# Filter pass of a four-layer graph network: attributes as three bf16 parts, bf16 transposes and first layer, index loads that wait for gathers

## The reference

```python
def _L2_gnn_ref(x, edge_index, edge_attr, W1, b1, W2, b2, Ws, bs, Wn, bn):
    src, dst = (edge_index[0], edge_index[1])
    h = jax.nn.relu(edge_attr @ W1.T + b1)
    w = h @ W2.T + b2
    msg = w * x[src]
    agg = jax.ops.segment_sum(msg, dst, num_segments=x.shape[0])
    return jax.nn.relu(x @ Ws.T + bs + agg @ Wn.T + bn)
```

## Time and profile before

| | us |
|---|---|
| median of three runs (8740.71 to 8760.54) | 8757.48 |
| the profiled execution's own time | 8686.3 |
| its span, first to last instruction | 8684.5 |
| TensorE busy | 5822.4 (67%) |
| VectorE busy | 4301.2 (50%) |
| POOL busy | 3273.6 (38%) |
| ScalarE busy | 1758.3 (20%) |

### The profile page before, as it was taken

The page is one execution under the profiler, slowest core; times in us unless marked ns, Lnnn a source line. Parts: engine busy times, 40 slices in busy tenths (PEclk is TensorE's granted clock), DMA queues, the critical chain, the costliest instruction groups (busy, mean ns, idle before and its releaser), DMA issues. The chain is left out here.

```text
span 8684.5 us, 135899 instructions
## 1 busy us (share of the span) xinstructions
PE 5822.4 (67%) x29812; PEld 4117.1 (47%) x29813; DVE 4301.2 (50%) x14700; ACT 1758.3 (20%) x3520; POOL 3273.6 (38%) x3354
## 2 busy tenths in 40 slices
PE   4313666794555554555454778888878888889999
PEld 4312443573333333333332455555555555677877
DVE  7877777424666666666666233333333333432222
ACT  0013888202111111111112111111111111110000
POOL 0105000004555555555552555555555555300000
PEclk9856777897777777777777566556665656689999
DMA  1231332553333333333332222222222222256666
GB/s 31 102 100 61 107 103 100 187 221 75 71 72 70 71 69 71 71 70 71 71 69 31 43 34 34 35 34 35 35 34 34 35 35 35 23 207 246 255 240 232
DMA packets 1052581, 764.66 MB, mean 88 GB/s; under 512 B 868977, under 2 KB 978241, under 8 KB 1032914
## 3 DMA queue, kind: packets, MB, share of 16 engines
q1 hardware_dynamic: 664738, 483.03, 18.4%
q0 software_dynamic: 131808, 243.11, 11.8%
q10 hardware_dynamic: 255904, 37.09, 2.5%
HBM read 657.77 MB, written 143.22 MB: 92 GB/s over the span
## 5 line engine op out<-in xcount | busy, mean ns | idle before, releaser
L1874 POOL DMA_INDIRECT rows<-node_rows,idx_ring x1612 | 1528.9, 948 | 1201.8 <-DMA idx_ring<-src_all 707.7
L1874 POOL DMA_INDIRECT rows<-node_rows_wide,idx_ring x1612 | 1545.9, 959 | 1099.9 <-DMA idx_ring<-sorted_pairs 574.3
L1923 PE MATMUL ps_sum<-hots,act_ring 128*97 128x128 f32 x3224 | 647.2, 365 | 1281.2 <-DVE hots L1908 530.2
L1911 DVE TENSOR_SCALAR hots<-iota,lane_all 128x128 f32<-128x128 f32 x1612 | 462.9, 288 | 1807.3 <-remote 1250.0
L1923 PEld LDWEIGHTS ps_sum<-hots,act_ring 128*97 128x97 f32 x3224 | 545.9, 230 | 1579.0 <-DVE accT L1917 1107.3
L1923 PE MATMUL ps_sum<-hots,msg 128*96 128x128 f32 x3224 | 722.6, 399 | 397.6 <-DVE hots L1911 194.1
L1386 PE MATMUL ps_conv<-conv_rows,adj_ring 128*128 128x288 bf16 x7497 | 942.5, 288 | 44.3 <-DVE conv_rows L1345 22.0
L1917 DVE TENSOR_TENSOR accT<-accT,ps_sum 97x128 f32 (+1 forms) x3224 | 908.3, 282 | 49.3 <-issue 16.7
L1386 PEld LDWEIGHTS ps_conv<-conv_rows,adj_ring 128*128 128x128 f16 x7497 | 738.3, 99 | 233.3 <-issue 23.1
L2031 PEld LDWEIGHTS ps_w<-w2w,hid 97*128 97x128 f32 x3224 | 581.8, 271 | 530.8 <-issue 475.5
L1950 PE MATMUL ps_e<-w1e,aT 128*128 128x384 f32 x1612 | 817.9, 644 | 18.0 <-DVE aT L1986 15.5
(11 more groups left out here) (341 smaller groups left out, 6088.8 us busy)
## 6 DMA issues: line engine op xcount, KB each, us to landing
adj_ring<-adjacency SPq DMA_DIRECT2D x144, 2176.0 KB, 7.8
adjacency<-panels SPq DMA_DIRECT2D x588, 128.0 KB, 1.7
idx_ring<-sorted_pairs SPq DMA_DIRECT2D x1612, 1.0 KB
attr_ring<-sorted_attr ACTq DMA_DIRECT2D x1612, 16.0 KB
rows<-node_rows_wide,idx_ring POOLq DMA_INDIRECT x1612
attr_ring<-sorted_attr SPq DMA_DIRECT2D x1612, 8.5 KB
rows<-node_rows,idx_ring POOLq DMA_INDIRECT x1612
sorted_attr<-in_edge_attr SPq DMA_DIRECT2D x5, 5000.0 KB
```

Of the source, the lines that this page charges most:

```text
L1874: g.indirect_dma_start(out=rows[:, r, j, 0:width], out_offset=None, in_=table, in_offset=bass.IndirectOffsetOnAxis(ap=idx, axis=0)).then_i ...
L1911: last = v.tensor_scalar(hots[:, r % 2, j, :], iota[:, :], lane, None, ALU.is_equal)
L1923: last = pe.matmul(ps_sum[0:M, r % 2, j, :], what(r, j), hots[:, r % 2, j, :], start=True, stop=True)
```

## The change

All of it is in the filter pass.

- VectorE makes three bf16 parts of each attribute group (`split_attributes`): the attributes rounded to bf16, the rest of that rounded, and the rest of that, into `attr_parts`, so that their sum is the fp32 value to about 24 bits. The four operations are chained by `attr_cut` and end with `attr_split`. The step has lag 0 on VectorE and stands last in a turn.
- The transposes become ordinary matmuls of 128 x 54 bf16 with a bf16 identity; `ps_t` and `aT` have 54 rows (18 attributes in three parts), and `aT` is bf16.
- The first layer becomes three bf16 matmuls over 54 rows, one for each bf16 part of the weights, which stand three times under one another in `w17`. The parts of the weights are made once ahead of the loop.
- All other lags grow by one.
- SP's index load waits for the landing of the gather of six groups back (`gathered`), not for the product; its attribute loads wait for `attr_split` of six groups back. POOL waits for the indices and then for the product of six groups back.

```diff
-        w17 = sbuf("w17", [KB, D])
+        w17 = sbuf("w17", [KS, D])
...
-                        past(sp, rows_used, q - (GPI - 1))
+                        if SPLIT_WAITS:
+                            if not isinstance(turn, int) or turn > 0:
+                                sp.wait_ge(gathered[r].sem, base[gathered[r]] + turn * (16 * G))
+                                sp.sem_inc(passed_s.sem, 1)
+                        else:
+                            past(sp, rows_used, q - (GPI - 1))
...
                         if kind == "filter":
+                            past(sp, attr_split, q - (GPI - 1))
+                            sp.sem_inc(passed_s.sem, 1)
                             attributes(sp, SP, q, r)
...
                         g.sem_inc(gather_go.sem, 1)
+                        if SPLIT_WAITS:
+                            past(g, rows_used, q - (GPI - 1))
+                            g.sem_inc(passed_g.sem, 1)
...
+                def split_attributes(v, q, turn, r):
+                    v.wait_ge(attr_ready[r].sem, base[attr_ready[r]] + (turn + 1) * (16 * G))
+                    past(v, attrT, q - 1)
+                    parts, of, rest = attr_parts[:, r % 2], attr_ring[:, r], attr_rest[:, r % 2]
+                    v.sem_inc(passed_v.sem, 1)
+                    v.tensor_copy(parts[:, :, 0, :], of).then_inc(attr_cut.sem, 1)
+                    past(v, attr_cut, q * 3 + 1)
+                    v.tensor_tensor(rest, of, parts[:, :, 0, :], ALU.subtract).then_inc(attr_cut.sem, 1)
+                    past(v, attr_cut, q * 3 + 2)
+                    v.tensor_copy(parts[:, :, 1, :], rest).then_inc(attr_cut.sem, 1)
+                    past(v, attr_cut, q * 3 + 3)
+                    v.tensor_tensor(parts[:, :, 2, :], rest, parts[:, :, 1, :], ALU.subtract).then_inc(attr_split.sem, 1)
...
-                        last = pe.transpose(ps_t[0:kk, r % 2, j * P:(j + 1) * P], attr_ring[:, r, j, :],
-                                            ident[:, :])
+                        last = pe.matmul(ps_t[0:KS, r % 2, j * P:(j + 1) * P],
+                                         attr_parts[:, r % 2, j].rearrange("p k f -> p (k f)"), ident_h[:, :],
+                                         start=True, stop=True)
...
-                            pe.matmul(ps_e[0:D, r % 2, :], w17[:, :], aT[:, r % 2, :], start=True,
-                                      stop=True).then_inc(edge_mm.sem, 1)
+                            for k in range(3):
+                                last = pe.matmul(ps_e[0:D, r % 2, :], w17_parts[:, k, :], aT[:, r % 2, :], start=(k == 0),
+                                                 stop=(k == 2))
+                            last.then_inc(edge_mm.sem, 1)
...
-                        turns(pe, [(lambda q, t, r: transposes(pe, q, t, r, KB), 0), (layer1, 1), (layer2, 2),
-                                   (lambda q, t, r: sum_targets(pe, q, t, r, lambda r, j: msg[:, r % 3, j, :]), 4)])
+                        turns(pe, [(lambda q, t, r: transposes(pe, q, t, r), 1), (layer1, 2), (layer2, 3),
+                                   (lambda q, t, r: sum_targets(pe, q, t, r, lambda r, j: msg[:, r % 3, j, :]), 5)])
...
-                        turns(v, [(lambda new, old: hots_and_adds(v, new, old), 4, 5), (times, 3)])
+                        turns(v, [(lambda new, old: hots_and_adds(v, new, old), 5, 6), (times, 4), (split_all, 0)])
```

More of the change, by code:

```diff
@@ L110 @@
 EPS = 1e-5
+SPLIT_KIND = "filter"
+KS = 3 * KB
 class Signal:
@@ L271, in graph_kernel @@
         passed_t = sem("passed_t")
+        passed_s = sem("passed_s")
+        passed_g = sem("passed_g")
+        attr_split = sem("attr_split")
+        attr_cut = sem("attr_cut")
+        filter_w = sem("filter_w")
         cast = Signal(top, nc, "cast")
@@ L409, in _ @@
                         (lnb[:, :], w["L1_gnn_ln_b"].to_broadcast([P, D])),
-                        (w17[0:EB, :], w["L2_gnn_W1"]), (w17[EB:KB, :], w["L2_gnn_b1"]),
                         (w2w[0:D, :], w["L2_gnn_W2"]), (w2w[D:D + 1, :], w["L2_gnn_b2"]),
@@ L418, in _ @@
                     ]
+                    for k in range(3):
+                        loads.append((w17[k * KB:k * KB + EB, :], w["L2_gnn_W1"]))
+                        loads.append((w17[k * KB + EB:(k + 1) * KB, :], w["L2_gnn_b1"]))
                     for j in range(G):
@@ L2042, in relu, with split_all @@
                             a.activation(hid[0:D, r % 2, :], ps_e[0:D, r % 2, :], ACT.Relu).then_inc(edge_act.sem, 1)
-                        turns(a, [(lambda q, t, r: keep_attrT(a, q, t, r, KB, edge_mm), 0), (relu, 1)])
+                        turns(a, [(lambda q, t, r: keep_attrT(a, q, t, r), 1), (relu, 2)])
                     @block.vector
                     def _(v):
+                        def split_all(q, turn, r):
+                            split_attributes(v, q, turn, r)
                         def times(q, turn, r):
```

29 lines of the change are left out of this document (21 added, 8 removed).

## The result

The changed kernel takes 8925.7 us (median of four, 8893 to 8999), the kernel before, in the same comparison, 8758.1: a ratio of 1.0212, 95% interval 1.0164 to 1.0259. Forecast were 8482 us and a gain of 3%.

A forecast was written before the change was run, and what follows sets the result against it. TensorE, busy 82% of the filter pass, was taken as the fullest engine; 403 groups times (0.72 - 0.02) is 282, less 7 one-off, 275 us saved: 8686.3 to 8411, plus 71.2 is 8482 us, range 8150 to 8840.

The forecast's parts named there:

- The work of TensorE: Filter pass, transposes and first layer: 0.41 and 0.44 us saved at the lower clock, weighed 0.72 us a group.
- VectorE's parts: Filter pass, VectorE: two casts and two subtractions add 1.00 us a group, mostly hidden; 0.02 counted as cost.
- The rival of a cast that waits for a whole gather instruction: VectorE's casts beside gathers: blocked casts cost 0.40 us a group, leaving 114 us saved, 8643 us; chance 0.07.
- The step that failed first: Filter pass, TensorE: savings on the engine busy 82% count in full, 0.72 us a group, with idle time unchanged.
- the idle 1.24 us: TensorE's standstill per group in the filter pass, nearly all ahead of the sums; assumed to stay as it is.
- 70% of groups at the lower level and 30% at the upper: TensorE's clock in the filter pass: turns of 6.46 us and 3.46 us, used to weigh the savings.
- Wrong would be the forecast above all if the clock moved: TensorE's clock in the filter pass: each tenth of groups going from 5.6 to 3.0 us gives 105 us.
- The second step that failed: POOL's new waits in the filter pass: product to gather shrinks from 2.6 to about 0.3 us, directly worth 0.
- the sums are held by the gathers: Filter pass: sooner gathers catch the sums' signals; three in four caught gives 7.18 us a group, 8913 us; chance 0.18.
- its turning point: Held-sums rival, filter pass: slower than before once 49% of groups are caught, at 7.54 us against 6.11.
- a turn without a gap in the trace of before: TensorE in the filter pass: a 6.46 us turn with sums answered in time, taken as evidence against held sums.
- POOL as the bound: Filter pass: gathers set the period at 5.3 us a group, 8155 us; chance 0.19.

The follow-up runs named there:

- Experiment 1: The changed kernel with the old waits, so the bf16 parts alone, against the kernel before: 1.0010 and 1.0015 with no signal held, 1.0037 with signals held.
- Experiment 2: The kernel before with the new waits alone, no bf16 parts, against the kernel before: 0.9998, 0.9998 and 0.9985 with no signal held, 1.0162 with signals held.
- after_again: The changed kernel, unedited, measured again beside the kernel before, with signals held: 8870 us against 8695, ratio 1.0198.
- before_new_waits_5: The kernel before with the new waits alone and no bf16 parts, with signals held: 8842 us against 8690 for the kernel before, ratio 1.0162.
- parts_old_waits_3: The changed kernel with the old waits, so the bf16 parts alone, with signals held: 8724 us against 8689 for the kernel before, ratio 1.0037.

## Why the prediction was wrong, point by point

**The work of TensorE was sized right.** At the lower clock level the transposes take 0.56 us (6013.14 to 6013.70, forecast 0.58) and the first layer 1.44 (to 6015.14, forecast 1.51). Here are these rows of the changed kernel, TensorE in order of time, which answer to the earlier trace rows:

```profile
6013.14 0.63 PE L1969 MATMUL ps_t<-ident_h,attr_parts 128*54 128x128 bf16 x4
...
6013.70 1.51 PE L2063 MATMUL ps_e<-aT,w_parts 54*96 54x512 bf16 x3
...
6015.14 1.17 PE L2071 MATMUL ps_w<-w2w,hid 97*128 97x96 f32 x4
```

Together 0.94 us less a turn, forecast 0.85.

**VectorE's parts were sized right.** From the first cast to the end of the last subtraction 0.95 us (6001.28 to 6002.23), forecast 1.00. The casts take 209 ns in the mean. The rival of a cast that waits for a whole gather instruction falls, and with it the Trainium skill's rule as I applied it (page "SBUF — State Buffer", section "Who interferes with whom": a cast in the mode that takes the shared ports, and a gather, block each other): these rows show casts of usual length beside and inside a gather.

```profile
6001.28 0.18 DVE L1957 CAST attr_parts<-attr_ring 128x72 bf16<-128x72 f32 x1
...
6001.37 0.94 POOL L1899 DMA_INDIRECT rows<-node_rows,idx_ring  x1 [0.30 <-issue]
...
6001.77 0.20 DVE L1961 CAST attr_parts<-attr_rest 128x72 bf16<-128x72 f32 x1
```

Something of it shows all the same. The 106 casts of this pass that start 0.5 to 0.8 us after a gather's start take 0.30 us in the mean and up to 0.44; the other 696 take 0.19 and never over 0.22. The subtractions, 0.23 us at either place, do not change. So a gather stretches a cast for a part of its time, by up to 0.26 us and not by up to the 0.95 of the rival.

**The step that failed first** is "these steps stand on the engine that is busy 82%, so I count them in full, and leave the idle 1.24 us as they are". A busy share of 82% is no proof that the engine sets the period. The loop of the table in the experiments does: the next one-hots wait for the sums' signal, the next sums for the one-hots. TensorE's other work is in it only as far as it delays sums whose one-hots are ready, 2.76 us less the 1.7 of the one-hots and additions themselves. Experiment 1 shows 0.20 us of the 0.72 there, and 0.32 given back in the two other legs. The idle time was not a constant to be left standing; it is where the signals are late.

**The clock went the other way.** I weighed 70% of groups at the lower level and 30% at the upper. With the parts, TensorE has longer pauses and spends less time at the upper level: 0.61 to 0.58 with the parts alone, 0.56 with both. Sums and second layer, untouched, cost 130 us more. "Wrong would be the forecast above all if the clock moved" was the right worry, at more than half of the work saved in the two edited steps (230 us).

**The second step that failed** is "so directly this is worth nothing" for the new waits. I priced the 2.3 us by which a gather starts sooner at 0 on the main line and left the rest to a rival. Experiment 2 shows a loss of 1.6% for these waits alone. Two of its terms failed with it. SyncE does not run ahead: its loads are slowed beside the gathers, and in the profiled execution the index load ended every one of the 199 gaps. And where the product does release a gather, it starts 0.79 us later, not 0.3.

**The rival that came true** is "the sums are held by the gathers", at 7.18 us a group and 8913 us; measured are 7.18 (result) and 7.20 (after_again), from one-hots to the next one-hots as in the table, and 8926. Its mechanism is right: half of the gathers took the hold away. Its bookkeeping is not, and that the number fits so well is luck. I took the share of caught sums as what the change raises, to three in four; it stays at about half, and what grows is the length of a held answer, from 3.8 to 5.0 us. With one half caught its own sum would have given 6.11 + 0.5 x 1.43 = 6.83, no change. And its turning point leaned on 6.11 us for the uncaught groups, which nothing shows. I gave it 0.18, because a turn without a gap in the trace of before seemed to speak against it, where the rows of one held answer and 1250 us of unassigned wait spoke for it on the whole pass.

**POOL as the bound** is wrong here and right in the free condition, where the versions traced with either half of the change run at its 5.0 us a group (forecast for the rival: 5.3), and neither half is worth anything.

**What stays open.** Why the old waits let a caught sum be answered 7.3 us after the start of a burst and the new ones only after its end; the sums end at about the same point of a burst in both (4.0 to 4.8 us after its start in some of the cycles of before_new_waits_5, whose one-hots start at 11.5). SyncE's attribute loads do not tell the two apart: 64 and 62% of them are issued inside a burst with the old waits (before, parts_old_waits_3), 53 and 45% with the new ones (before_new_waits_5, the changed kernel). A version that halves them on SyncE did not help, and the runs that leave them out never met the held condition. Whether it is the number of gathers or the length of a burst that holds a signal is open too, and so is what sets the condition. No version that computes everything beats the kernel before by more than 0.2%, in either condition; the lowest ratio of one that computes everything in the held condition was that of the parts with the old waits, 1.0037.

## What to carry to other kernels

Before an operation is taken off the busiest engine, close the loop: take the two steps that wait for each other from group to group and add up work and waiting between them. If the waits in it are for signals that come late and not for work, less work buys little. An unassigned wait ("remote") of a thousand microseconds deserves an explanation before any forecast, and a wait that is moved so that a transfer starts sooner should be priced by what then runs beside it, not by its own length. And an instruction that ends just before another starts has not always released it: compare the distance with the usual one (here 0.27 us where 0.79 is needed), or look which of its waits the engine's queue passes last.

## What the hardware showed that I had not expected

Signals of TensorE, SyncE's instructions and some of VectorE's register instructions are slow while indirect gathers run, in one condition and not in the other: four attribute loads 7.17 us against 1.92, register instructions 0.7 us against 0.04, sums answered 5.0 us late against 0.15 to 0.2 in quiet time. The updates by VectorE's products, one-hots and additions and by ScalarE's work stand 0.01 us behind their instructions, in either condition. In the other condition the same programs take 7360 us, not 8700, with copies of `ps_t` starting 0.04 us after the transposes in the median and 0.11 at the ninetieth percentile. That is 15% of the time, more than any edit here moved.

The clock follows the rhythm of the waits: with half of the gathers left out the same instructions of TensorE ran at 0.88 of full speed instead of 0.56, and its busy time in the pass fell from 2198 to 1483 us without one matmul less.
